# Low parts of the first feed-forward's weights dropped from the attention/feed-forward kernel

## What is computed

```python
x = x + mlstm_cell(layernorm(x), ctx, ctx, gate weights...)        # stage A: 8 heads, causal, gated by an exponential of cumulated gates
x = x + swiglu(layernorm(x), w_gate, w_up, w_down)                 # stage B: 256 -> 768 -> 256, integer weights -127..127 times 1/127
x = x + cross_attention(layernorm(x), ctx, mask, W, diagonal)      # stage C: relu projections, softmax over 128
x = x + ternary_ffn(layernorm(x), w1, w2, h1, h2, w3 with scales)  # stage D: 256 -> 1024 -> 1024 -> 1024 -> 256
```

## Time and profile before

| | us |
|---|---|
| median of 3 runs (620.58 to 622.68) | 622.67 |
| the profiled execution, its own time | 623.7 |
| its span, first to last instruction | 622.1 |
| PE busy in the span | 555.4 |
| DVE busy | 354.3 |
| ACT busy | 213.4 |
| POOL busy | 92.4 |

### The profile page before, as it was taken

The page is one execution under the profiler, slowest core; times in us unless marked ns, Lnnn a source line. Parts: engine busy times, 40 slices in busy tenths (PEclk is TensorE's granted clock), DMA queues, the critical chain, the costliest instruction groups (busy, mean ns, idle before and its releaser), DMA issues.

```text
span 622.1 us, 8968 instructions
## 1 busy us (share of the span) xinstructions
PE 555.4 (89%) x2728; PEld 449.4 (72%) x2728; DVE 354.3 (57%) x851; ACT 213.4 (34%) x372; POOL 92.4 (15%) x112
## 2 busy tenths in 40 slices
PE   0458979886899999889999999999999999999994
PEld 0335747565688888766888887888878888888884
DVE  5627999967777776874524346344463344543222
ACT  1203333313566683333512226112253122341120
POOL 5212453421600004310000010000100000100001
PEclk9858989877899999997999999999999999999998
DMA  5553644543784658760000000000000000000000
GB/s 148 130 163 72 180 74 129 127 130 114 270 306 141 198 106 280 187 158 2 1 0 2 1 35 1 0 2 0 18 17 0 0 0 0 34 0 0 0 0 34
DMA packets 57752, 47.57 MB, mean 76 GB/s; under 512 B 37278, under 2 KB 48542, under 8 KB 57316
## 3 DMA queue, kind: packets, MB, share of 16 engines
q1 hardware_dynamic: 52108, 28.34, 17.7%
q0 software_dynamic: 5616, 18.88, 9.3%
HBM read 40.58 MB, written 2.10 MB: 69 GB/s over the span
## 4 chain that ended last, share of the span: by engine, by line
PE 67%; DVE 3%; issue 2%; ACT 1%; POOL 0%; DVEq 0%; ACTq 0%; POOLq 0%
PE ps L788 51%; PE ps L564 5%; PE ps L567 3%; PE ps L566 2%; PE ps L552 2%; DVE xn L1084 1%; PE ps L759 1%; PE ps L558 1%; PE ps L560 1%; ACT al L1012 1%; PE ps L559 1%; PE ps L773 1%; ACT h L1047 0%; DVE sc L1325 0%; DVE x L1296 0%
## 5 line engine op out<-in xcount | busy, mean ns | idle before, releaser
L788 PE MATMUL ps<-hBt,h 128*128 128x512 f32 x512 | 117.4, 390 | 0.0
L788 PE MATMUL ps<-hA,h 128*128 128x512 f32 x512 | 117.2, 390 | 0.0
L788 PEld LDWEIGHTS ps<-hA,h 128*128 128x128 f32 x512 | 95.9, 188 | 20.3 <-DVE hA L1371 0.4
L788 PEld LDWEIGHTS ps<-hBt,h 128*128 128x128 f32 x512 | 95.8, 188 | 20.2 <-DVE hBt L1371 0.4
L1047 ACT ACTIVATE h<-ps,scol 128x512 f32<-128x512 f32 x64 | 44.1, 690 | 175.4 <-PE ps L788 175.2
L788 PE MATMUL ps<-xT,w 128*128 128x512 f32 x256 | 60.6, 396 | 0.3 <-issue 0.3
L788 PEld LDWEIGHTS ps<-xT,w 128*128 128x128 f32 x256 | 46.6, 190 | 13.6 <-DVE h L1366 2.3
L1386 DVE CAST hBt<-h 128x512 fp32r<-128x512 f32 x32 | 13.7, 427 | 73.7 <-ACT h L1047 73.7
L1386 DVE CAST hA<-h 128x512 fp32r<-128x512 f32 x32 | 13.7, 427 | 70.0 <-ACT h L1047 70.0
L407 POOL TENSOR_TENSOR rstd<-ve,mhalf 128x4 f32<-128x4 f32 x16 | 16.4, 1023 | 249.4 <-DVE ve L1079 249.3
L564 PE MATMUL ps<-xT,l 128*128 128x512 f32 x96 | 40.4, 421 | 4.8 <-issue 2.6
(11 more groups left out here) (169 smaller groups left out, 930.2 us busy)
## 6 DMA issues: line engine op xcount, KB each, us to landing
looked<-w_all_in SPq DMA_DIRECT2D x16, 704.0 KB, 4.6
h<-w_all_in POOLq DMA_DIRECT2D x16, 512.0 KB, 7.1
V<-ctx_in SPq DMA_DIRECT2D x32, 128.0 KB, 4.5
Qb<-xT SPq DMA_DIRECT2D x64, 64.0 KB, 2.5
w<-w_all_in POOLq DMA_DIRECT2D x3, 1024.0 KB, 7.0
x<-x_in SPq DMA_DIRECT2D x4, 512.0 KB, 4.0
kstA<-ctxT_in SPq DMA_DIRECT2D x4, 512.0 KB, 5.9
kstC<-ctxT_in SPq DMA_DIRECT2D x4, 512.0 KB, 5.8
```

The costliest lines, as they stand in the source:

```text
L788: last = mm(o, a, b, start=(k == 0 and p == 0), stop=(k == n_k - 1 and p == 1))
```

## The change

- `l0` and `l0d` lose their low half. `lows` only writes the low part of `xaw`, in the halves with u = 0; a new semaphore `raw_here` says that the raw weights of a group are there, and ACT's `low_sum` and PE's stage B wait for it (PE waits for `l0_lo` only ahead of stage C).
- The general branch of stage B takes the raw float32 weights from `rawgu` and `rawd`, with the activations' two parts read as float32; both branches now do two matmuls for a product (`both`). In the branch that the shown inputs take, the matmuls and their operands are those of before.
- So `rawgu` and `rawd` must last until stage B ends. `low_sum` writes its output to a tile `unused`; three of the four `looked` pieces move to the room of the dropped low parts and the fourth to the end of `w3`; and POOL waits for `down_done` before the loads of `w1`, `w2`, `w3` instead of behind them.

```diff
@@ -111,14 +110,13 @@
         rawgu = place([ring_at[0]], "rawgu", [P, 2, KD, HB], F32)
-        looked = place([ring_at[0]], "looked", [P, FLAG_BUFS, FLAG_W], F32)
-        assert FLAG_BUFS * FLAG_W <= 3 * KD * HD
         ring = place(ring_at, "ring", [P, RING, MD, P], F32)
...
         assert rawd_at[0] <= base[0]
+        w_end = base[0]
         xT = place(base, "xT", [P, 2, 2, KD, GT], F32R)
@@ -161,8 +159,14 @@
         r1 = [work]
-        l0 = place(r1, "l0", [P, 2, 2, KD, HB], F32R)
-        l0d = place(r1, "l0d", [P, 2, MB, D], F32R)
+        l0 = place(r1, "l0", [P, 2, KD, HB], F32R)
+        l0d = place(r1, "l0d", [P, MB, D], F32R)
+        lows_at = [r1[0]]
+        unused = place([r1[0]], "unused", [P, 2 * HB], F32)
+        looked = [place(lows_at, f"looked{m}", [P, FLAG_W], F32) for m in range(FLAG_BUFS - 1)]
+        looked.append(place([w_end - 6 * HD], f"looked{FLAG_BUFS - 1}", [P, FLAG_W], F32))
+        r1[0] += (2 * KD * HB + MB * D) * 4
+        assert lows_at[0] <= r1[0] and FLAG_W * 4 <= 6 * HD
         kT = place(r1, "kT", [P, 2, 2, KD, GT], F32R)
@@ -220,7 +224,7 @@
         names = """x_first x_second x_rest ident_ld gw_ld consts mask_ld mask_free hi_ld
-            raw_seen gw_lo gw_cast const_set mv_ready rstd_ready xn_ready tr_done xhi_done xlo_done x_free
+            raw_here raw_seen gw_lo gw_cast const_set mv_ready rstd_ready xn_ready tr_done xhi_done xlo_done x_free
             khi_done klo_done gate_done gate_copied gate_moved ab_ready ln_ready ncs_ready er_ready z_ready
@@ -334,7 +338,7 @@
                     sp.wait_ge(s["flag_used"], FLAG_BUFS * g + m + 1)
-                    sp.dma_start(looked[:, m, :], w_all_in[:, bass.ds((FLAG_BUFS * g + m) * FLAG_W, FLAG_W)])\
+                    sp.dma_start(looked[m][:, :], w_all_in[:, bass.ds((FLAG_BUFS * g + m) * FLAG_W, FLAG_W)])\
                         .then_inc(flag_ld[m], 16)
@@ -430,30 +434,23 @@
                 gu = (slice(None), bass.ds(i, 1), u)
-                pool.dma_start(l0[:, 0, bass.ds(i, 1), u, :], l0gu_in[gu]).then_inc(s["hi_ld"], 16)
+                pool.dma_start(l0[:, bass.ds(i, 1), u, :], l0gu_in[gu]).then_inc(s["hi_ld"], 16)
                 pool.dma_start(rawgu[:, bass.ds(i, 1), u, :], l0gu_in[gu]).then_inc(s["hi_ld"], 16)
...
                     m = bass.ds(i * (MB // 2), MB // 2)
-                    pool.dma_start(l0d[:, 0, m, :], l0d_in[:, m, :]).then_inc(s["hi_ld"], 16)
+                    pool.dma_start(l0d[:, m, :], l0d_in[:, m, :]).then_inc(s["hi_ld"], 16)
                     pool.dma_start(rawd[:, bass.ds(i, 1), :, :].rearrange("p a m w -> p (a m) w"), l0d_in[:, m, :])\
...
-            def lows(i, u):
-
-                nc.gpsimd.tensor_tensor(l0[:, 1, bass.ds(i, 1), u, :], rawgu[:, bass.ds(i, 1), u, :],
-                                        l0[:, 0, bass.ds(i, 1), u, :], ALU.subtract).then_inc(s["l0_lo"], 1)
-                if u == 0:
-                    nc.gpsimd.tensor_tensor(xaw[:, 1, bass.ds(i, 1), :], rawx[:, bass.ds(i, 1), :],
-                                            xaw[:, 0, bass.ds(i, 1), :], ALU.subtract).then_inc(s["l0_lo"], 1)
-                else:
-                    m = bass.ds(i * (MB // 2), MB // 2)
-                    nc.gpsimd.tensor_tensor(l0d[:, 1, m, :], rawd[:, bass.ds(i, 1), :, :],
-                                            l0d[:, 0, m, :], ALU.subtract).then_inc(s["l0_lo"], 1)
+            def lows(i):
+
+                nc.gpsimd.tensor_tensor(xaw[:, 1, bass.ds(i, 1), :], rawx[:, bass.ds(i, 1), :],
+                                        xaw[:, 0, bass.ds(i, 1), :], ALU.subtract).then_inc(s["l0_lo"], 1)
@@ -479,7 +476,9 @@
                     pool.wait_ge(s["hi_ld"], 64 * (g + 1))
-                    lows(i, u)
+                    pool.sem_inc(s["raw_here"], 1)
+                    if u == 0:
+                        lows(i)
                     h_root(Q * g + 1, 1)
@@ -498,13 +497,13 @@
             pool.wait_ge(s["flag_sums"], 2)
+            pool.wait_ge(s["down_done"], Q * G)
             pool.dma_start(w1[:, :, :], w_all_in[:, SEC_W1:SEC_W2].rearrange("p (k f) -> p k f", k=KD))\
...
                 .then_inc(s["w_ld"], 16)
-            pool.wait_ge(s["down_done"], Q * G)
             with pool.Fori(0, 2) as i:
@@ -559,12 +558,10 @@
-            def two(o, lhs, rhs, first, last, weight_moves=False):
+            def both(o, lhs, rhs, first, last):
...
                 mm(o, lhs(0), rhs(0), start=first, stop=False)
-                if weight_moves:
-                    return mm(o, lhs(1), rhs(0), start=False, stop=last)
-                return mm(o, lhs(0), rhs(1), start=False, stop=last)
+                return mm(o, lhs(1), rhs(1), start=False, stop=last)
@@ -668,13 +665,21 @@
-            pe.wait_ge(s["l0_lo"], NRAW)
+            pe.wait_ge(s["raw_here"], G)
             pe.wait_ge(s["c_ready"], UN * G + 2)
...
             def stage_b(general):
-                by = three if general else two
+                def up_w(a, c, m):
+                    at = slice(m * P, (m + 1) * P)
+                    return rawgu[:, a, c, at] if general else l0[:, a, c, at]
+
+                def down_w(k):
+                    return rawd[:, k // (MB // 2), k % (MB // 2), :] if general else l0d[:, k, :]
+
+                def seen(view):
+                    return view.bitcast(F32) if general else view
                 with pe.Fori(0, 2) as i:
@@ -685,9 +690,8 @@
                                 for c in range(KD):
-                                    last = by(ps[:, bank + m % 2, :],
-                                                 lambda p: l0[:, p, a, c, m * P:(m + 1) * P],
-                                                 lambda p: xT[:, u, p, c, :], c == 0, c == KD - 1)
+                                    last = both(ps[:, bank + m % 2, :], lambda p: up_w(a, c, m),
+                                                lambda p: seen(xT[:, u, p, c, :]), c == 0, c == KD - 1)
                             last.then_inc(s["gu_done"], 1)
@@ -695,8 +699,9 @@
                                     pe.wait_ge(s["hlo_ready"], MB * g + k + 3)
-                                last = by(ps[:, OB + q % 2, 0:D], lambda p: hB[:, p, k, q * S:(q + 1) * S],
-                                          lambda p: l0d[:, p, k, :], k == 0, k == MB - 1, weight_moves=True)
+                                last = both(ps[:, OB + q % 2, 0:D],
+                                            lambda p: seen(hB[:, p, k, q * S:(q + 1) * S]),
+                                            lambda p: down_w(k), k == 0, k == MB - 1)
                             if k == MB - 1:
@@ -740,6 +745,7 @@
+            pe.wait_ge(s["l0_lo"], KD)
             pe.wait_ge(s["flag_sums"], 2)
@@ -902,10 +908,10 @@
-            def low_sum(view, to, name):
+            def low_sum(view, to, name, over=None):
...
                 low = view.bitcast(U16).rearrange("p (w a) -> p w a", a=2)[:, :, 0:1]
-                fn(view.rearrange("p (w a) -> p w a", a=1), low, ACT.Copy, accum_out=to).then_inc(s[name], 1)
+                fn((view if over is None else over).rearrange("p (w a) -> p w a", a=1), low, ACT.Copy, accum_out=to).then_inc(s[name], 1)
@@ -947,12 +953,12 @@
-                            act.wait_ge(s["l0_lo"], 2 * g + 2)
+                            act.wait_ge(s["raw_here"], g + 1)
                             low_sum(rawgu[:, bass.ds(i, 1), u, :].rearrange("p a w -> p (a w)"),
-                                    facc[:, bass.ds(2 * g, 1)], "raw_seen")
+                                    facc[:, bass.ds(2 * g, 1)], "raw_seen", unused[:, 0:HB])
                             if u == 1:
                                 low_sum(rawd[:, bass.ds(i, 1), :, :].rearrange("p a m w -> p (a m w)"),
-                                        facc[:, bass.ds(2 * g + 1, 1)], "raw_seen")
+                                        facc[:, bass.ds(2 * g + 1, 1)], "raw_seen", unused[:, HB:2 * HB])
                             if u == 0:
@@ -969,7 +975,7 @@
                 act.wait_ge(flag_ld[m], 16 * (g + 1))
-                low_sum(looked[:, m, :], facc[:, bass.ds(FLAG_BUFS * g + m + 2 * G, 1)], "flag_used")
+                low_sum(looked[m][:, :], facc[:, bass.ds(FLAG_BUFS * g + m + 2 * G, 1)], "flag_used")
             with act.Fori(0, 2) as i:
```

More of the change, by code:

```diff
@@ L46 @@
 CONSTS = 16 * 10
-NRAW = 2 * G
 W_ALL = 2 * KD * HD + MD * D + 2 * MD * HD
```

## The result

The changed kernel takes 619.8 us (median of 9 runs, 615.44 to 621.52) against 622.67 for the kernel before, measured beside it (9 runs, 620.58 to 624.42). The medians differ by 2.9 us, 0.5%. The ratio worked out over all runs is 0.9939, with a 95% interval of 0.9911 to 0.9967, so 2.1 to 5.5 us: the changed kernel is faster, if by little.

What follows compares the result with a forecast made beforehand. DVE's order was taken to set the pace in stage A, PE in stage B. Gains of 1.03 + 1.48 + 1.39 + 1.62 = 5.52 us, all else zero, took 622.67 to 617.2 us; range 614.6 to 620.4.

Steps and rivals of the forecast that it cites:

- What holds DVE up: Stage A: POOL's subtractions stop DVE instructions that read two SBUF operands until they end; without them L1121 takes 0.28 us.
- the choice between rule and row: Groups 0 and 2: by the skill's rule L451 blocks L1121, sum 5.5 us; if harmless like L407, 6.5. It took 5.5.
- the ends that it says coincide within 0.2 us: Against the rival that subtractions only seem to cost: four DVE ends coincide with POOL's within 0.2 us.
- Groups 0 to 2: 3.90 forecast: Stage A's gate blocks, subtractions gone: gains of 1.03, 1.48 and 1.39 us in groups 0, 1 and 2.
- a rival: Absorbed in group 3: PE's wait for queries at 127.01 swallows the 3.90 us, leaving 1.62, so 621.0; chance 0.12.
- Group 3: 1.62 forecast: End of stage A: L620 moves from 141.90 by only 0.92, and DVE's L1178 starts at about 143.0 instead of 144.62.
- its upper bound for group 3: At most all of group 3's 2.12 us, and another 1.08 if the second L620 runs in 2.02.
- Stage D: zero forecast: Matmuls: the branch not taken only makes the program longer, by an unknown amount; counted as zero.
- from 163 us on every stage has its old length: Sign to look for in the timeline after: no stage from 163 us on changes its length.
- The rival: Slower by the jump: a longer skipped branch before stage B's first matmul costs more instruction waits; four give 625.2; chance 0.05.
- The earlier wait for `down_done`: POOL before the w1, w2, w3 loads: met 2.7 us before POOL gets there, so zero cost.
- the forecast's upper bound of 8.04: Most the subtractions could give: 6.96 us with L1121 clean in three groups, plus 1.08 from the second L620.

Runs made afterwards that it cites:

- e9: The kernel before, unchanged, profiled a second time; one run, 621.14 us.
- e6: The kernel before without POOL's subtractions for l0 and l0d in groups 1 and 3 (four left out): 617.31 us, ratio 0.9917.
- e10: The changed kernel, unchanged, profiled a second time; one run, 616.88 us.
- e8: e4 with two `k_lo` moved behind stage B's first outputs, the `h1` loads ahead of them and POOL's loop written out: 610.6 us, ratio 0.9812.
- e2: The kernel before with 96 never-run matmuls (192 instructions) added behind the loop in stage B's skipped branch: 626.85 us, ratio 1.0054.
- e3: The changed kernel with 32 more never-run matmuls (64 instructions) behind the loop in stage B's skipped branch: 614.76 us, ratio 0.9869.
- e4: The changed kernel with stage D's two branches exchanged, the taken one first: 615.46 us, ratio 0.9863.

## Why the prediction was right where it was, and where it failed

**What holds DVE up: right, to the hundredth.** The subtractions stop DVE instructions with two SBUF inputs until they end. The times came out as forecast: L1121's 0.28 in group 1, its 0.73 and 0.69 beside `xaw` (0.7 to 0.8), and 0.48 and 0.47 for L1153 and L1159 in group 3. That decides the choice between rule and row too: `xaw`'s subtraction blocks, so 5.5 was the right one of 5.5 and 6.5. POOL fell by 11.4 (11.0 forecast). The forecast gave both L451 0.76; the one in group 2 took 1.16 before and 0.72 after, which is the other 0.4. Of the ends that it says coincide within 0.2 us, three do; those of L1153 and L1159 come some 0.3 after POOL's.

That 1.16 is a case the other way round, and it stands in e9 and e6 too. DVE's L1153, with two SBUF inputs, ran inside L451 in its usual 0.47, and L451 is the one that got longer:

```profile
110.53 1.16 POOL L451 TENSOR_TENSOR xaw<-rawx,xaw  x1
...
110.64 0.47 DVE L1153 SCALAR_TENSOR_TENSOR hm<-hm,hmv,lns 128x256 f32<-128x256 f32 x1
```

**Groups 0 to 2: 3.90 forecast, 2.2 and 3.2 measured** (column "1st to 10th", 64.4 in all four executions with the subtractions, 62.2 and 61.2 after). Each subtraction's own price was right. From the 1st to the 2nd `hrs` it is 1.08 less (1.03 forecast), from the 5th to the 6th 1.48 (1.48), from the 9th to the 10th 1.45 (1.39), the same in both profiles after. In between, 0.86 and 0.92 were lost again in the first profile, 0.31 and 0.42 in e10. Something was absorbed, as a rival had it, but at another place than its queries of group 3. DVE came earlier in group 1 and met POOL's `k_lo` more fully, 0.94 before and 1.31 after (and once more at the next `k_lo`: 0.93 before, 1.44 after); first the kernel before, then after:

```profile
68.53 2.37 POOL L422 TENSOR_TENSOR kT<-kstA,kT 128x1024 fp32r<-128x1024 f32 x1
...
70.25 0.94 DVE L1153 SCALAR_TENSOR_TENSOR hm<-hm,hmv,lns 128x256 f32<-128x256 f32 x1
77.19 0.27 DVE L1099 TENSOR_SCALAR fmn<-gf,gb 32x128 f32<-32x128 f32 x1 [0.19 <-DMA gf<-gsb]
```

```profile
68.07 2.38 POOL L426 TENSOR_TENSOR kT<-kstA,kT 128x1024 fp32r<-128x1024 f32 x1 [0.35 <-ACT kT L893]
...
69.42 1.31 DVE L1159 SCALAR_TENSOR_TENSOR hm<-hm,hmv,lns 128x256 f32<-128x256 f32 x1
...
77.23 0.27 DVE L1105 TENSOR_SCALAR fmn<-gf,gb 32x128 f32<-32x128 f32 x1 [0.68 <-DMA gf<-gsb]
```

and the gate transfers, waited for 0.19 before, were now waited for 0.68: of group 0's microsecond 0.2 is left at 77 us, counted from the first `hrs`. No run takes this `k_lo` away, so how the loss divides between the two stays open.

**Group 3: 1.62 forecast, more measured.** Its own subtractions are worth more than was said: from the stall to the end of A it takes 19.5 to 20.2 us with them and 17.0 to 18.1 without, in the mean 19.85 against 17.6, so 2.2. The step moved L620 by the first wait only, and kept the second wait of 2.13, which fell to 1.09; its upper bound for group 3, 2.12 and 1.08, holds the 2.2. On top comes the stall at the queries: in two of four executions with all subtractions and in e6, in none of the others, some 3 us each time. So the 6.3 between the first two profiles is not a size of the change: the second pair differs by 4.5 (142.40 to 137.86), and at B's first root the means are 101.7 for the four with all subtractions and 95.5 for the five without any (e8 left out): 6.1 us, where the forecast had 5.5. The parts: 2.5 (64.4 to a mean of 61.9), 1.4 (17.4 to 16.0), 2.2. The 1.4 hangs on two stalls in four executions, so the 6.1 is loose by about as much.

**Stage D: zero forecast, 3.1 measured; this is the step that failed.** It was put as "the branch not taken gets other ones; it only makes the program longer, by an amount that this trace does not show", and "I take zero", with "from 163 us on every stage has its old length". The rival looked for the price at the jump into stage B, and said that length would be paid there. That wait was 2.56 and 2.35 in the two profiles before, 2.11 and 3.44 in those after, and 1.9 to 4.2 in all twelve, with no relation to the length of the skipped branch; from the last weighted sum's start to stage B's first matmul it took 5.7 and 6.1 us before, and 5.7 and 6.1 after. The price is paid 300 us later, at the turn of another loop, and it follows from the placement. From C's end to D's last root it is 228.4 and 229.3 us in the two profiles before and 232.0 and 231.9 in those after: 3.1 more, of it 2.4 at the turn and the rest in "C's end to D", which spreads from 63.5 to 66.1 whatever the place. In the medians the same place costs 4.0 (e2) and 5.0 (after against e3), more than the 1.9 and 2.4 that the turns show; e2's interval, 1.7 to 5.0, holds both, and where a further cost would sit stays open.

**The moves.** The earlier wait for `down_done` cost nothing, as argued: the `w` loads go out at 229.31 after 235.29, by the 6.0 us that all else moved. PE's matmul count stayed at 2728, as said.

**The sum.** Forecast 5.5 gained; found 6.1 in stage A, less 3.1 in stage D: 3.0, beside 2.9 between the medians. The mechanism of stage A was right, the number 617.2 was 2.6 too low for a reason that the forecast had dismissed, and that 619.8 lies inside the range is in part luck: the price of the placement was in no term of the sum. Where no layout is in the way the change is worth 7.4 to 8.1 (e4, e3), near the forecast's upper bound of 8.04 and more than the landmarks explain. Some 1.5 us of it can be the start of stage B, 22.5 in e3 and e10 but 23.9 in after, which differs from execution to execution. Whether the rest is more than the spread of the runs stays open.

## What to carry to other kernels

When a change adds or removes instructions, in skipped code too, every long loop behind it (here 1,657 instructions a turn) comes to lie elsewhere: compare the instruction queue's packets before and after, and shift the loop by padding before judging the change (putting the taken branch first did as well here, once). A long operation on POOL that streams SBUF cost 4 us where DVE had a run of SBUF instructions that PE waited for; look for a place where DVE works from PSUM or waits. And profile the same kernel twice before giving a name to a difference of 2 to 3 us between two profiles.

## What the runs showed of the hardware

- Instructions that never run cost 4.0 us in 192 (ratio 1.0054) and nothing in 256 (0.9995); in the changed kernel, 64 more on top of its 192 took 5.0 us away. The cost shows as `issue` before the first matmul of the loop's second pass (1.60 to 2.21 us), and as 25 packets of instructions in place of 15.
- A POOL tensor_tensor of 128x1024 stretches DVE's tensor_scalar 128x256, which has one tensor input, too: four take 5.51 us in place of 1.38 (e4 and e8). Blocking is not kept to DVE instructions with two SBUF tensors. The Trainium skill (SBUF — State Buffer, "Who interferes with whom") counts `tensor_scalar` among the operations that can take the shared ports without a second SBUF input, when their operands allow a 2-port mode; the trace agrees, and the forecast had quoted only the rule on two inputs.
- After a wait of about 2 us for the same transfer PE went on at a granted clock of 0.55 in one execution and of 1.00 in another; the three executions with the low clock there (before, e2, e6) took some 3 us longer from the 10th to the 13th `hrs`.
